# Rotated attention with normalised queries and keys: norms broadcast by DMA from DRAM in place of a matmul that spreads them

## What is computed

```python
q, k, v = split(x @ Wqkv)              # 16 heads of 64, n = 512, two batches
q = l2norm(q) * qs; k = l2norm(k) * ksc
q = q * cos * scale + rotate_half(q) * sin * scale
k = k * cos / scale + rotate_half(k) * sin / scale
out = local_attention(q, k, v)         # windows of 32, softmax(8 * q.k)
return out @ Wo
```

## Time and profile before

| | value |
|---|---|
| median of 3 runs | 2305.04 us (2300.93 to 2308.49) |
| profiled execution, its own time | 2303.67 us |
| its span, first to last instruction | 2301.9 us |
| mean granted TensorE clock | 0.845 |
| busy share PE / DVE / ACT / POOL | 80% / 58% / 38% / 25% |
| DMA queue of the kernel's transfers | 107.80 MB, 13.9% of 16 engines |

### The profile page before, as it was taken

How to read it: one execution, slowest core, us unless ns; L and a number is a source line. 1 busy time by engine, 2 the same in 40 slices (tenths; PEclk the granted TensorE clock), 3 DMA queues, 4 the chain that set the end, 5 groups by cost and what they waited for, 6 DMA issues and landing times.

```text
span 2301.9 us, 44158 instructions
## 1 busy us (share of the span) xinstructions
PE 1837.2 (80%) x15373; PEld 968.6 (42%) x15373; DVE 1330.0 (58%) x2266; ACT 878.1 (38%) x1541; POOL 582.6 (25%) x548
## 2 busy tenths in 40 slices
PE   6973233589888898867688989889888898989888
PEld 2552111346465464522243534535444353543434
DVE  6655676555364563632565566656647565674665
ACT  2341111322514325133343535444444453554445
POOL 3430000000000000000154254424516434451552
PEclk9985555797978989777788989898898998989889
DMA  5200000000000000000312132030212213113120
GB/s 196 72 29 1 0 0 2 19 7 9 15 6 9 6 9 15 0 1 1 121 50 99 39 110 85 17 137 11 99 60 88 99 38 110 52 50 107 41 99 11
DMA packets 41602, 110.30 MB, mean 48 GB/s; under 512 B 13440, under 2 KB 16128, under 8 KB 40256
## 3 DMA queue, kind: packets, MB, share of 16 engines
q1 hardware_dynamic: 41408, 107.80, 13.9%
HBM read 28.34 MB, written 0.52 MB: 13 GB/s over the span
## 4 chain that ended last, share of the span: by engine, by line
PE 45%; DVE 19%; issue 17%; ACT 10%; POOL 8%; DMA 1%; DVEq 0%; ACTq 0%; POOLq 0%; SPq 0%
PE ps L364 4%; PE ps L1102 4%; POOL big L528 4%; PE ps L266 3%; POOL big L511 3%; PE ps L271 3%; PE ps L277 3%; PE ps L306 3%; PE ps L354 2%; DVE big L459 2%; PE ps L1160 2%; PE ps L1127 2%; PE ps L338 2%; PE ps L1143 2%; PE ps L1478 2%
## 5 line engine op out<-in xcount | busy, mean ns | idle before, releaser
L518 POOL TENSOR_TENSOR big<-big 128x512 f32<-128x512 f32 x112 | 142.3, 1270 | 1422.1 <-DMA big<-big 1421.9
L528 POOL TENSOR_TENSOR big<-big,nm 128x384 f32<-128x384 f32 x224 | 184.2, 844 | 232.9 <-DVE nm L500 232.9
L458 DVE TENSOR_TENSOR big<-ps,big 128x512 f32<-128x512 f32 x224 | 153.9, 687 | 95.5 <-ACT sq L396 73.5
L306 PE MATMUL ps<-rs,big 32*128 32x512 f32 x384 | 143.6, 832 | 71.7 <-ACT rs L407 61.6
L429 ACT ACTIVATE big<-big 128x384 f32<-128x384 f32 x224 | 110.6, 523 | 219.9 <-DVE big L489 219.9
L338 PE MATMUL ps<-ident,big 128*128 128x128 f32 x896 | 143.7, 299 | 26.9 <-POOL big L528 19.7
L486 DVE TENSOR_REDUCE nm<-ps 128x4 f32<-128x384 f32 x224 | 114.5, 552 | 66.0 <-PE ps L324 65.6
L459 DVE TENSOR_TENSOR big<-ps,big 128x512 f32<-128x512 f32 x224 | 152.5, 681 | 0.0
L436 ACT ACTIVATE big<-ps 128x512 f32<-128x512 f32 x224 | 122.0, 585 | 55.2 <-PE ps L338 51.1
L519 POOL TENSOR_TENSOR big<-big 128x512 f32<-128x512 f32 x112 | 142.3, 1271 | 0.0
L1354 DVE TENSOR_TENSOR big<-ps,fix 128x512 f32<-128x512 f32 x192 | 119.4, 684 | 32.6 <-PE ps L1102 28.9
(11 more groups left out here) (238 smaller groups left out, 3271.3 us busy)
## 6 DMA issues: line engine op xcount, KB each, us to landing
big<-big SPq DMA_DIRECT2D x280, 256.0 KB, 2.4
big<-in_F_w SPq DMA_DIRECT2D x6, 1536.0 KB, 6.0
big<-big SPq DMA_DIRECT2D x42, 128.0 KB, 3.0
big<-in_D_w SPq DMA_DIRECT2D x18, 256.0 KB, 2.6
big<-in_F_wo SPq DMA_DIRECT2D x6, 512.0 KB, 6.9
big<-in_F_w SPq DMA_DIRECT2D x6, 341.0 KB, 3.1
big<-in_A_w SPq DMA_DIRECT2D x1, 1536.0 KB, 9.3
big<-in_F_w SPq DMA_DIRECT2D x6, 192.0 KB, 2.9
```

Of the source, the lines that this page charges most:

```text
L306: pe.matmul(ps[:, k, :], spr[r:r + 32, p // 2, :], rn[r:r + 32, :], start=True, stop=True, tile_position=(r, 0))\
L458: dve.tensor_tensor(tmp[:, i, w, :], ps[:, k, :], tb[:, 2 * w, :], ALU.mult).then_inc(*part.mark((key, b, p, 0)))
L518: pool.tensor_tensor(Q[:, p, :], tmp[:, i, 0, :], swp[:, i, 0:T], ALU.add).then_inc(*roped.mark((key, b, p)))
L528: pool.tensor_tensor(v, v, nm[:, p % 3, 16 + 4 * h:20 + 4 * h].unsqueeze(2).to_broadcast([128, 4, KW]), ALU.mult)\
```

## The change

The inverse norms `rn` (128x512, f32, 256 KB) are stored once per batch to a DRAM tensor `norms`, and from there each pair's two rows for q, and then for k, are read back so that row 0 fills partitions 0 to 63 and row 1 partitions 64 to 127, into the `sinp` slot of pair p (free again by then). All of this is issued by SyncE, after it has waited for `n_ready` and for the last `k_added` of the batch. GpSimd then multiplies both `Q` and `KT`. TensorE, ScalarE and VectorE lose their parts of the spreading. GpSimd's multiplications run two pairs ahead of its scaling, not one. The `spr` matrix and `knr` go away.

```diff
-        def a_spread_pe(pe, key, b, p):
...
-        def a_k_norm_act(act, key, b, p):
...
-        def a_q_norm_dve(dve, key, b, p):
...
+        rn_out = nc.dram_tensor("norms", (128, T), F32, kind="Internal").ap()
...
+        def norm_wait(eng, b, p):
+
+            uses = len([i for i in range(NP) if i % 3 == p % 3])
+            at = 32 * (uses * b + p // 3 + 1)
+            eng.wait_ge(spread_in[p % 3], Loop.reg * (32 * B * uses) + at)
...
                 a_proj_pe(pe, key, b, src(b), l2)
-                if l2:
-                    a_spread_pe(pe, key, b, 0)
                 for p in range(NP + 2):
-                    if l2 and p + 1 < NP:
-                        a_spread_pe(pe, key, b, p + 1)
...
-        def a_k_raise_pool(pool, key, b, p):
-            pool.wait_ge(*k_norm.at((key, b, p)))
+        def a_raise_pool(pool, key, b, p):
+            norm_wait(pool, b, p)
             pool.wait_ge(*k_added.at((key, b, p)))
-            pool.tensor_tensor(KT[:, p, :], KT[:, p, :], knr[:, p % 2, :], ALU.mult).then_inc(*k_raised.mark((key, b, p)))
+            pool.tensor_tensor(Q[:, p, :], Q[:, p, :], sinp[:, p % 3, 0:T], ALU.mult).then_inc(*q_norm.mark((key, b, p)))
+            pool.tensor_tensor(KT[:, p, :], KT[:, p, :], sinp[:, p % 3, T:2 * T], ALU.mult).then_inc(*k_raised.mark((key, b, p)))
...
                 if l2:
-                    a_k_raise_pool(pool, key, b, 0)
+                    a_raise_pool(pool, key, b, 0)
+                    a_raise_pool(pool, key, b, 1)
                 for p in range(NP):
-                    if l2 and p + 1 < NP:
-                        a_k_raise_pool(pool, key, b, p + 1)
+                    if l2 and p + 2 < NP:
+                        a_raise_pool(pool, key, b, p + 2)
                     pool.wait_ge(*inverted.at((key, b, p)))
...
+                if key == "F":
+                    a_norm_sp(sp, key, b)
+
+        def a_norm_sp(sp, key, b):
+
+            sp.wait_ge(*n_ready.at((key, b)))
+            sp.wait_ge(*k_added.at((key, b, NP - 1)))
+            sp.dma_start(rn_out, rn).then_inc(rn_stored, 16)
+            sp.wait_ge(rn_stored, Loop.reg * (16 * B) + 16 * (b + 1) if Loop.now else (16 * B) * (LAYERS - 1) + 16 * (b + 1))
+            for p in range(NP):
+                if p >= 3:
+                    sp.wait_ge(*k_raised.at((key, b, p - 3)))
+                for w in range(2):
+                    r = 32 * (2 * (p % 2) + w) + 2 * (p // 2)
+                    sp.dma_start(sinp[:, p % 3, T * w:T * w + T], rn_out[r:r + 2, :].unsqueeze(1).to_broadcast([2, 64, T])).then_inc(spread_in[p % 3], 16)
...
-            pe.wait_ge(f_const, 48)
+            pe.wait_ge(f_const, 32)
...
-            for dst, name in ((tab0, "tabF"), (ssel, "ssel"), (spr, "spr")):
+            for dst, name in ((tab0, "tabF"), (ssel, "ssel")):
```

More of the change, by code:

```diff
@@ L221, in build @@
         rn = rs[:, 1, :]
-        knr = ar(2, T)
         ssel = ar(4, 32)
-        spr = ar(4, 128)
         scl = ar(2)
@@ L237, in build @@
         guarded, n_ready = sg("guarded"), sg("n_ready")
-        q_norm, k_norm, k_raised = sg("q_norm"), sg("k_norm"), sg("k_raised")
+        q_norm, k_raised = sg("q_norm"), sg("k_raised")
         topped, subbed, exped, added, inverted = sg("topped"), sg("subbed"), sg("exped"), sg("added"), sg("inverted")
@@ L243, in build @@
         swapped = [raw(f"swapped{i}") for i in range(3)]
+        spread_in = [raw(f"spread_in{i}") for i in range(3)]
+        rn_stored = raw("rn_stored")
+        rn_out = nc.dram_tensor("norms", (128, T), F32, kind="Internal").ap()
         def slot(b, p):
@@ L419, in attn_act @@
                 a_proj_act(act, key, b, l2)
-                if l2:
-                    a_k_norm_act(act, key, b, 0)
                 for p in range(NP + 2):
-                    if l2 and p + 1 < NP:
-                        a_k_norm_act(act, key, b, p + 1)
                     if p < NP:
@@ L476, in attn_dve @@
                 a_proj_dve(dve, key, b, l2)
-                if l2:
-                    a_q_norm_dve(dve, key, b, 0)
                 for p in range(NP):
-                    if l2 and p + 1 < NP:
-                        a_q_norm_dve(dve, key, b, p + 1)
                     s4 = lambda h: ps[:, h, 0:4 * KW].rearrange("p (j k) -> p j k", j=4)
@@ L1602, in f_dve @@
                 shift_dve(dve, b, (moved, 1))
-            dve.wait_ge(f_const, 48)
+            dve.wait_ge(f_const, 32)
             with layers(dve, "F") as L:
@@ L1780, in more @@
     a["ssel"] = (np.arange(32)[None, None, :] == 2 * pr[None, :, None] + i[:, None, None] // D).astype(np.float32)
-    a["spr"] = (i[:, None, None] % 32 == 2 * pr[None, :, None] + i[None, None, :] // D).astype(np.float32)
 def kernel(**inp):
```

## The result

The changed kernel took 3004.06 us (median of 4 runs, 3002.46 to 3006.80) beside 2306.73 us for the kernel before: a ratio of 1.303, 95% interval 1.3003 to 1.3057. The forecast was 3056 us. The profiled execution's span is 2999.8 us, 697.9 more than before, at a mean granted clock of 0.751 (0.845 before).

A forecast was written before the change was run, and what follows sets the result against it. It took a GpSimd-TensorE-VectorE cycle, 4.62 us a pair, to pace the loop. With loads on two engines, 2.5 + 1.8 + 86.4 + 2.5 + 20 = 113.2 us replace 50.5; twelve times 62.7 gives 3056 us, range 2958 to 3210, widened below to 2945.

The forecast's parts named there:

- landings of 7 us and more: Sign that the forecast is right: loads from `norms` land that late, the later ones of a pair later still.
- The rule of the Trainium skill: Engines per transfer: largest number up to 16 dividing the outermost non-trivial dimension of both access patterns; the lowest-numbered ones.
- Store: Start of each batch: SyncE stores 256 KB of norms and waits for the landing, 2.5 us.
- Loads: Each batch: fixed part 1.8 us, then sixteen loads of 5.4 us back to back on two engines, 86.4 us.
- The last two products: End of each batch: the last pair's two multiplications on GpSimd, 2.5 us.
- The part after the last products: Scores of pair 7 to the output's addition (L504): 15.0 us at full clock, 20 with the clock's addition.
- the lower reading of 5.2: Cost of one 256 KB load on two engines, us, derived from the output store's 20.7 engine-us for 512 KB.
- 5 on top for the clock: Last part of each batch: 5 us added because TensorE begins the last pair at half clock; bounds 0 and 12.
- Sixteen engines: Rival: each load takes 0.65 to 0.8 us; start +6.05 a batch less 2.4 for the loop, 2348 us; chance 0.09.
- The two loads on different engines: Rival: a pair's two loads use separate engines, 5.4 us a pair, +16.5 a batch, 2502 us; chance 0.03.
- The loop's gain: Pair loop, pairs 3 to 7: spread leaves, GpSimd sets 4.15 us a pair instead of 4.62, 2.4 us a batch.
- Faster: Rival: pair loop gives back mean 5.8 us a batch, more than the start's 5.1, so 2295 us; chance 0.01.

The follow-up runs named there:

- e1_wide: Changed kernel, each load cut to fill 64 partitions with one head's q and k rows, 64 copies outermost on both sides: 2364.19 us, ratio 1.0253.
- e3_one_load: Changed kernel without the load of the key norms, both products using the query norms: 2500.23 us (one run).
- e5_hybrid2: Changed kernel with 64-copy loads, store issued before the last `k_added` wait, and TensorE spreading norms of pairs 0 and 1: 2270.15 us, ratio 0.9855.

## Why the prediction was right

**The mechanism** held in its main steps: two engines (12.9% of 16), shared by both loads of a pair, the loop set by them, GpSimd idle before every first product with DMA as the releaser. TensorE's clock was granted at 0.50 before the loop and 0.61 in it, so it was at half clock for part of the time. The landings of 7 us and more that I had named as a sign can't be read, since the profile gives no landing for these loads. The rule of the Trainium skill ("DMA: Bandwidth & Descriptors", section "Why a DMA increments its semaphore by 16 and not by 1") was what the trace of before could not give; by that rule, the traces agree, with two engines for two rows at 50 GB/s, four for four at 101, and both loads on the same ones.

**The terms**, for batch 1 of layer 5. Store: 2.5 foreseen, 2.06 measured (2552.69 to 2554.75). Loads: 1.8 + 86.4 = 88.2 foreseen, 86.8 measured (2554.75 to 2641.52); in the seven intervals after the first a load costs 73.71 / 14 = 5.26 us, against 5.4. The last two products: 2.5 and 2.5. The part after the last products: 20 foreseen, 18.5 measured (2644.01 to 2662.55). Together 109.9 against 113.2. Over all 12 batches the mean is 109.2, and before it was 50.7 (I had taken 50.5 from one layer). So 12 x 58.5 = 702 us where I had 752, and 698 in the spans. The forecast is 52 us too high, nearly all of it in these small terms, all of which erred the same way; a load's 5.26 is nearest the lower reading of 5.2, from the output's store.

**The last part was right by luck.** I had 15 us from the scores of pair 7, and 5 on top for the clock. TensorE's timeline shows something else:

```profile
2643.97 3.18 POOL L496 TENSOR_TENSOR big<-big,nm 128x384 f32<-128x384 f32 x4
```

```profile
2644.92 1.95 PE L331 MATMUL ps<-ident,big 128*128 128x128 f32 x8 [5.09 <-POOL big L496]
2646.80 1.86 PE L347 MATMUL ps<-big 128*64 128x64 f32 x32
2648.59 0.50 PE L310 MATMUL ps<-band,identb 128*128 128x384 bf16 x2
```

The scores of pair 7 (L310) begin 4.6 us after the last product, not at once; from there to the addition it is 14.0 us, at a granted clock of 1.00 from 2649 on. Over the 12 batches the two parts are 4.57 and 13.96 us; before they were 0.57 and 15.04. What stands in between is program order. On GpSimd the scaling of pair 5 (L496) is queued behind the products of pair 7, because the change runs the products two pairs ahead: the reciprocals of pair 5 were done at 2632.20, its scaling began at 2643.97. On TensorE the transposes of pair 5 and the values of pair 4 stand before the scores of pair 7. The clock costs some of it, 1.95 and 1.86 us for these two against 1.44 and 1.15 before, 1.2 us in all where I had 5. So the term is 14.0 + 4.6 and not 15 + 5. No run here moves the scaling ahead, so what that would be worth is not shown.

**The rivals.** *Sixteen engines* was tested by e1_wide, 2364 where I had 2348. The failed term is the landing of a wide load, 2.4 taken from the swaps, 4.4 measured; the swaps go to every second partition, these loads to a block of 64. *The two loads on different engines* was excluded by e3_one_load. The loop's gain was right. *Faster*: I had given it 0.01 and asked for a start that costs less than the loop gives back. That is what e5_hybrid2 builds, by taking the first two pairs out of the DMA's way, and it gives 34 us where e1_wide loses 60. The loop's gain, foreseen as 2.4 us a batch and lost behind the transfers in the changed kernel, is 2.4 and 2.0 there, and the end gives 0.3 and 0.8 more, once nothing is paid for it at the start.

## What to carry to other kernels

Before a transfer is put on a path, look at the outermost dimension of both its sides: a source of two rows repeated 64 times each ran on two of sixteen engines, 5.3 us for 256 KB, and the page's mean DMA share of 15% hid it; a share that stays flat at 1/8 in a stretch, with issue times of 5 us, is the sign. Latency that a loop hides well may still be paid in full at its start, so price the first item and the steady state apart, and let the old way serve the first items.

## What the runs showed that I had not expected

A wide load of 256 KB from DRAM into 64 neighbouring partitions took 4.4 us to land (4.1 with distinct rows), at 15 to 16 GB/s for a busy engine, and 2.9 into all 128, at 22, while the same bytes between partitions, swapped two by two, took 2.4, at 25. A 0.69 us product moved from GpSimd (1.27 us there) to VectorE left the time the same within 0.1%, but as the sum of a shorter start and a longer loop, in which GpSimd's scalings grew from 1.61 to 2.08 us a pair. And a multiplication queued two pairs ahead on GpSimd held back a scaling whose input had been ready for 11.8 us.
